# Counting edges on 128 partitions in 157 tiles, instead of 125 partitions in 160 tiles

## The reference

```python
edge_index = jnp.stack([src, dst])
h = jnp.maximum(_layernorm(x, axis=-1), 0.0)
x = x + _L0_gnn_ref(h, edge_index, ...)      # agg = segment_sum(h[src], dst, num_segments=625)
...
x = x + _L1_gnn_ref(h, edge_index, ...)      # agg = segment_sum(h[col], row)
x = x + _L2_gnn_ref(h, edge_index, ...)      # 4 blocks of attention over the edges, and an MLP each
x = x + _L3_gnn_ref(h, edge_index, ...)      # 2 layers of attention over the edges, norms and an MLP
```

## Time and profile before

| | us |
|---|---|
| median of 3 runs (1119.16 to 1120.65) | 1120.2 |
| span of the profiled execution, first to last instruction | 1117.2 |
| first matmul of the counting | 6.08 |
| first matmul of the network behind the counting (L1220) | 123.50 |
| PE busy over the span | 1066.1 (95%) |

### The profile page before, as it was taken

The page is one execution under the profiler, slowest core; times in us unless marked ns, Lnnn a source line. Parts: engine busy times, 40 slices in busy tenths (PEclk is TensorE's granted clock), DMA queues, the critical chain, the costliest instruction groups (busy, mean ns, idle before and its releaser), DMA issues.

```text
span 1117.2 us, 20722 instructions
## 1 busy us (share of the span) xinstructions
PE 1066.1 (95%) x6808; PEld 987.7 (88%) x6808; DVE 773.4 (69%) x1535; ACT 577.6 (52%) x1032; POOL 673.3 (60%) x923
## 2 busy tenths in 40 slices
PE   7999999899999999999999999999999999999797
PEld 7899897699888999889998899987999879998795
DVE  7899867756658566575665756666778867777634
ACT  7999675455321553315543145433667637676340
POOL 3232447754577545875558755499656866478671
PEclk9999999999999999999999999999999999999899
DMA  5200011412021120211201212122201201021101
GB/s 129 31 1 1 7 38 58 149 58 86 1 86 49 58 86 1 78 56 59 86 1 55 78 48 77 69 83 75 66 1 43 71 4 45 1 76 39 38 1 46
DMA packets 40963, 56.92 MB, mean 51 GB/s; under 512 B 14312, under 2 KB 14812, under 8 KB 40735
## 3 DMA queue, kind: packets, MB, share of 16 engines
q1 hardware_dynamic: 40600, 55.37, 15.7%
q10 hardware_dynamic: 260, 0.21, 0.1%
HBM read 51.44 MB, written 4.12 MB: 50 GB/s over the span
## 4 chain that ended last, share of the span: by engine, by line
PE 79%; DVE 6%; POOL 5%; ACT 4%; issue 3%; DMA 2%; DVEq 0%; POOLq 0%; SPq 0%; PEldq 0%; ACTq 0%
PE ps L340 42%; PE ps L1768 8%; PE ps L362 8%; PE ps L786 5%; PE ps L2101 3%; PE ps L2028 3%; PE ps L2402 3%; POOL w_lo L380 2%; ACT away L737 1%; PE ps L2065 1%; PE ps L1259 1%; PE ps L1246 1%; PE ps L1742 1%; DMA w_raw<-L_gnn_wk 1%; PE ps L1220 1%
## 5 line engine op out<-in xcount | busy, mean ns | idle before, releaser
L380 POOL TENSOR_TENSOR w_lo<-w_raw,w_hi 128x512 fp32r<-128x512 f32 x152 | 204.8, 1348 | 12.7
L340 PE MATMUL ps<-yt_hi,w_hi 128*128 128x314 f32 (+2 forms) x640 | 201.8, 315 | 2.8 <-DVE yt_lo L2236 1.6
L340 PE MATMUL ps<-yt_hi,w_lo 128*128 128x314 f32 (+2 forms) x640 | 197.6, 309 | 0.0
L340 PE MATMUL ps<-yt_lo,w_hi 128*128 128x314 f32 (+2 forms) x640 | 197.3, 308 | 0.0
L459 POOL TENSOR_SCALAR prob<-prob,rinv 125x628 f32<-125x628 f32 x160 | 126.4, 792 | 105.2 <-DVE rinv L444 86.9
L403 ACT ACTIVATE pt_hi<-ps 125x625 fp32r<-125x625 f32 x160 | 109.2, 694 | 102.9 <-PE ps L362 101.7
L377 POOL TENSOR_SCALAR w_hi<-w_raw 128x512 fp32r<-128x512 f32 x152 | 97.7, 643 | 95.3 <-DMA w_raw<-L_gnn_wo 28.8
L340 PEld LDWEIGHTS ps<-yt_hi,w_hi 128*128 128x128 f32 x640 | 121.8, 190 | 5.9 <-issue 4.4
L340 PEld LDWEIGHTS ps<-yt_hi,w_lo 128*128 128x128 f32 x640 | 121.7, 190 | 0.0
L340 PEld LDWEIGHTS ps<-yt_lo,w_hi 128*128 128x128 f32 x640 | 121.5, 190 | 0.1
L786 PE MATMUL ps<-oh_s,oh_d 125*125 125x314 bf16 x800 | 111.4, 301 | 10.1 <-DVE oh_s L639 6.8
(11 more groups left out here) (325 smaller groups left out, 2787.2 us busy)
## 6 DMA issues: line engine op xcount, KB each, us to landing
w_raw<-L_gnn_m_w SPq DMA_DIRECT2D x8, 1024.0 KB, 5.4
w_raw<-L_gnn_W SPq DMA_DIRECT2D x6, 1024.0 KB, 5.4
w_raw<-L_gnn_wv SPq DMA_DIRECT2D x4, 1024.0 KB, 6.1
w_raw<-L_gnn_wq SPq DMA_DIRECT2D x4, 1024.0 KB, 5.4
w_raw<-L_gnn_wk SPq DMA_DIRECT2D x4, 1024.0 KB, 7.4
w_raw<-L_gnn_wo SPq DMA_DIRECT2D x4, 1024.0 KB, 6.4
w_raw<-L_gnn_Wv SPq DMA_DIRECT2D x2, 1024.0 KB, 5.5
w_raw<-L_gnn_Wq SPq DMA_DIRECT2D x2, 1024.0 KB, 5.6
```

Of the source, the lines that this page charges most:

```text
L340: ins = pe.matmul(out_ap, lhs(i, kk), rhs(j, kk), start=kk == 0 and n == 0, stop=kk == count - 1 and n == 2)
L380: pool.tensor_tensor(w[slot][1][:, kk, 0:cols], w_raw[slot][:, kk, 0:cols], w[slot][0][:, kk, 0:cols].bitcast(FP32), ALU.subtract).then_in ...
```

## The change

The lists are laid on 128 partitions. The first 127 get 157 edges each, 19939 in all, and the last one gets the other 61. The tiles are 128 x 160 still, but the columns 0, 1 and 2 are skipped: the first chunk begins at tile 3. So there are 157 tiles, and 29 of them in the first chunk.

- Each list is loaded by two DMAs on the queue that had one: 127 partitions x 157 columns (rows of 628 bytes), and 5 overlapping pieces of 32 entries into the last partition.
- Pads and repetitions in the last partition are marked: POOL makes a tile `absent` (a memset and an `affine_select`), which is 0 for an edge that counts and -1256 elsewhere. DVE adds it to `dst_i` while it makes `dstf`, by a `scalar_tensor_tensor` that takes the place of a `tensor_copy`. A pad's `oh_d` is then zero.
- ACT has the places 0, 2, 4, 6 of each group and DVE 1, 3, 5, 7 as well as all `oh_d`. With tile 3 as the first, DVE makes the first `oh_s` as it did before.
- All one-hots are 128 partitions high. The waits on used tiles are shifted by 3 tiles. POOL's eight numbers stay as they are, and count from tile 3.
- `offset` becomes -0.497 for -0.49.

```diff
-ET = E // R
 CHUNKS = 5
-CT = ET // CHUNKS
+EP = 128
+CT = 32
+ET = CHUNKS * CT
+FULL = -(-E // EP)
+SKIP = ET - FULL
+FRESH = 12
...
-    OHA = (1, 3, 5, 7)
+    OHA = (0, 2, 4, 6)
+    USED = slice(SKIP, ET)
...
+    def edge_rows(name):
+        return a[name][0:(EP - 1) * FULL].rearrange("(p t) -> p t", t=FULL)
+
+    def edge_row(name):
+        return bass.AP(a[name].tensor, LAST_ROW, [[E, 1], [FRESH, CHUNKS], [1, CT]])
...
     def count_sp(sp):
-        sp.dma_start(ids[0][:], a["src"].rearrange("(p t) -> p t", t=ET)).then_inc(s_dst, 16)
+        sp.dma_start(ids[0][0:EP - 1, USED], edge_rows("src")).then_inc(s_dst, 16)
+        sp.dma_start(chunked(ids[0][EP - 1:EP, :]), edge_row("src")).then_inc(s_dst, 16)
         sp.dma_start(x[:], a["x"].rearrange("(t p) f -> p t f", p=R)).then_inc(s_x0, 16)
...
     def count_act(act):
-        act.dma_start(ids[1][:], a["dst"].rearrange("(p t) -> p t", t=ET)).then_inc(s_ids, 16)
+        act.dma_start(ids[1][0:EP - 1, USED], edge_rows("dst")).then_inc(s_ids, 16)
+        act.dma_start(chunked(ids[1][EP - 1:EP, :]), edge_row("dst")).then_inc(s_ids, 16)
...
+        steps.done(pool.memset(absent[:], 0.0))
         steps.wait(pool)
+        pool.affine_select(out=chunked(absent[:]), in_=chunked(absent[:]), compare_op=ALU.is_ge, fill=-2.0 * W,
+                           base=8 * CT * (EP - 1) - 8 * REAL, pattern=[[-1, CHUNKS], [8, CT]],
+                           channel_multiplier=-8 * CT).then_inc(s_absent, 1)
...
     def count_dve(dve):
-        dve.wait_ge(s_ids, 16)
-        steps.done(dve.tensor_scalar(upper[:], ids[1][:], float(H2), None, ALU.is_ge))
-        dve.wait_ge(s_dst, 16)
-        dve.tensor_copy(dstf[:], ids[0][:]).then_inc(s_idf, 1)
+        dve.wait_ge(s_ids, 32)
+        steps.done(dve.tensor_scalar(upper[:, USED], ids[1][:, USED], float(H2), None, ALU.is_ge))
+        dve.wait_ge(s_dst, 32)
+        dve.wait_ge(s_absent, 1)
+        dve.scalar_tensor_tensor(out=dstf[:, USED], in0=absent[:, USED], scalar=1.0, in1=ids[0][:, USED],
+                                 op0=ALU.mult, op1=ALU.add).then_inc(s_idf, 1)
...
         for c in range(CHUNKS):
-            for o in range(OH):
+            for o in range(0 if c else SKIP, OH):
                 onehots(c * CT + o, o, c == 0)
```

More of the change, by code:

```diff
@@ L467, in build @@
     cnt_i = cnt[:].bitcast(I32)
[L468 to L473, removed]
-    OH = 8
-    oh_d = sb("oh_d", "qk", [R, OH, W], BF16, 1280)
-    oh_s = sb("oh_s", "qk", [R, OH, H2], BF16, 1280 + OH * W * 2)
-    OHA = (1, 3, 5, 7)
-    nsrcm = sb("nsrcm", "rows", [R, ET], FP32, 4480)
-    nsrcv = sb("nsrcv", "rows", [R, ET], FP32, 5120)
-    away = sb("away", "qk", [R, len(OHA), H2], BF16, 1280 + OH * W * 2 + OH * H2 * 2)
+    ids = [sb(n, "rows", [EP, ET], I32, skip) for n, skip in (("dst_i", 0), ("src_i", 640))]
+    dstf = sb("dstf", "rows", [EP, ET], FP32, 1280)
+    srcm = sb("srcm", "rows", [EP, ET], FP32, 2560)
+    srcv = sb("srcv", "rows", [EP, ET], FP32, 3200)
+    upper = sb("upper", "rows", [EP, ET], FP32, 3840)
+    node = sb("node", "qk", [EP, W], FP16)
+    OH = 8
+    oh_d = sb("oh_d", "qk", [EP, OH, W], BF16, 1280)
+    oh_s = sb("oh_s", "qk", [EP, OH, H2], BF16, 1280 + OH * W * 2)
+    OHA = (0, 2, 4, 6)
+    USED = slice(SKIP, ET)
+    SKIP_A = sum(o in OHA for o in range(SKIP))
+    SKIP_D = 2 * SKIP - SKIP_A
+    LAST_ROW = E - (CHUNKS - 1) * FRESH - CT
+    REAL = (EP - 1) * FULL - LAST_ROW
+    assert REAL == CT - FRESH - 1 and LAST_ROW >= 0
+    nsrcm = sb("nsrcm", "rows", [EP, ET], FP32, 4480)
+    nsrcv = sb("nsrcv", "rows", [EP, ET], FP32, 5120)
+    away = sb("away", "qk", [EP, len(OHA), H2], BF16, 1280 + OH * W * 2 + OH * H2 * 2)
     offset = sb("offset", "rows", [R, 1], FP32, 5760)
+    absent = sb("absent", "ot", [EP, ET])
     above = sb("above", "ot", [R, TILES, H2], I16)
@@ L571, in count_pool @@
         steps.done(pool.memset(neg_half[:], -0.5))
-        steps.done(pool.memset(offset[:], -0.49))
+        steps.done(pool.memset(offset[:], -0.497))
         steps.done(pool.memset(neg_one[:], -1.0))
@@ L634, in onehots @@
             if not first:
-                dve.wait_ge(s_ohu, tile - OH + 1)
+                dve.wait_ge(s_ohu, tile - (OH + SKIP - 1))
             dve.tensor_scalar(oh_d[:, o, :], node[:], dstf[:, bass.ds(tile, 1)], None,
@@ L680, in count_dve @@
             for o in range(OH):
-                onehots(c * CT + OH + o, o, False)
+                onehots(c * CT + OH + o, o, c == 0 and o < SKIP)
                 norms = NORM_AT.get(c, ())
@@ L728, in move, with onehots @@
                                scale=1 / PACK).then_inc(s_above, 1)
-        def onehots(c, j, first=False, which=range(len(OHA))):
+        def onehots(c, j, which=range(len(OHA))):
             for n in which:
                 o = OHA[n]
-                tile, nth = j * OH + (c * CT + o), j * len(OHA) + (c * (CT // OH) * len(OHA) + n)
+                tile = j * OH + (c * CT + o)
+                nth = j * len(OHA) + (c * (CT // OH) * len(OHA) + n - SKIP_A)
+                first = c == 0 and tile < OH + SKIP
                 if not first:
@@ L740, in onehots @@
                 if not first:
-                    act.wait_ge(s_ohu, tile - OH + 1)
+                    act.wait_ge(s_ohu, tile - (OH + SKIP - 1))
                 act.activation(oh_s[:, o, :], away[:, n, :], ACT.Relu, bias=srcv[:, bass.ds(tile, 1)],
@@ L745, in count_act @@
         for c in range(CHUNKS):
-            onehots(c, 0, c == 0, range(2))
+            onehots(c, 0, range(0 if c else SKIP_A, 2))
             if c > 0:
                 move(c - 1)
-            onehots(c, 0, c == 0, range(2, len(OHA)))
+            onehots(c, 0, range(2, len(OHA)))
             onehots(c, 1)
@@ L778, in count_pe, with ready @@
         GROUPS = CT // OH
[L780 to L783, removed]
+        def ready(c, j, o, by_act_too=True):
+            pe.wait_ge(s_oh, j * before[-1] + (c * GROUPS * before[-1] + before[o] - SKIP_D))
+            if by_act_too:
+                pe.wait_ge(s_oha, j * by_act[-1] + (c * GROUPS * by_act[-1] + by_act[o] - SKIP_A))
         def count(c, o, m, start=False, stop=False):
@@ L795, in count_pe @@
             FREE = range(3) if c else range(TILES)
-            for o in range(2):
-                ready(c, 0, o)
+            head = 0 if c else SKIP
+            for o in range(head, head + 2):
+                ready(c, 0, o, by_act_too=c > 0 or o > SKIP)
                 for m in FREE:
-                    ins = count(c, o, m, start=o == 0)
+                    ins = count(c, o, m, start=o == head)
             if c > 0:
@@ L805, in count_pe @@
             ins.then_inc(s_ohu, 2)
-            for o in range(2, OH):
+            for o in range(head + 2, OH):
                 edge_tile(c, 0, o)
@@ L813, in count_pe @@
                     edge_tile(c, GROUPS - 1, o, o == OH - 1)
-                pe.wait_ge(s_ohu, (c + 1) * CT)
+                pe.wait_ge(s_ohu, (c + 1) * CT - SKIP)
                 pe.sem_inc(s_cf, TILES)
```

14 lines of the change are left out of this document (8 added, 6 removed).

## The result

| | before | after |
|---|---|---|
| median, us (5 runs each on one chip) | 1120.05 | 1127.06 |
| lowest to highest | 1119.16 to 1120.65 | 1126.44 to 1129.5 |
| first matmul of the counting | 6.08 | 13.76 |
| first matmul behind the counting | 123.50 | 129.26 |
| span of the profiled execution | 1117.2 | 1127.7 |

The ratio is 1.0067 (95% interval 1.0056 to 1.0078): 7.0 us slower, where 4.4 were forecast. The profiled execution is after's slowest, 1129.5 us. Three terms carry the difference.

A forecast was written before the change was run, and what follows sets the result against it. PE's counting, behind a list load nothing can bypass, was taken as the bound. -2.0 + 5.85 + 0.1 + 0.08 + 0.2 + 0.13 = +4.4 us on 1117.2 gives 1121.6, plus 3.0 to the median: 1124.6; range 1122.0 to 1128.0.

The forecast's parts named there:

- hurt chunk ends: Rival: list late as forecast, and `w_lo` against `unpack` at three chunk ends costs up to 2.7 us; 1127.3; chance 0.10.
- dear rows: In the chunk-ends rival: list rows on the one engine at 0.032 us or above, giving 1128.2; that rival's chance 0.10.
- The three tiles, -2.0: In the first chunk of the counting: 15 matmuls fewer at 0.133 us each, all on the path, -2.0 us.
- The lists in 127 rows, +5.85: At the start: both lists go through one DMA engine, 254 rows at 0.0287 us, 7.29 us for 1.44.
- two bounds of this term: Load of the lists: +4.9 us with a row at 0.025 us, +6.7 with a row at 0.032.
- x and the weights behind it: Loads after the lists: x and weights land about 5.9 us later, as the counting does, so they cost nothing.
- The small transfers and the pads: At the start: each list's second transfer +0.1 us; DVE's `scalar_tensor_tensor` in place of `tensor_copy` +0.08 us.
- The ends of chunks, +0.2: Fifth tile's `oh_s` now comes from ACT behind `move`: four places at 0.05 us, +0.2 us (0 to 0.4).
- the last `oh_s`, +0.13: End of the counting: ACT's last `oh_s` is now the last tile but one's, so one more matmul follows the wait.
- POOL's pieces, 0: POOL's pieces come one tile before chunk ends rather than four, `w_lo` beside `unpack`: nothing; other end +2.7 us.
- C: Experiments' theory: PE's idle time behind the counting, at a certain time behind PE's start, sets off the half clock.

The follow-up runs named there:

- 113 + 12 rows: Kernel before, 125 partitions and 160 tiles, each list loaded in two transfers of 113 and 12 rows: 1126.7 us, ratio 1.0066.
- two of 157 tiles with filler: Changed kernel with lists in 112 + 15 rows, plus 12 useless matmuls in PE's idle time behind the counting, run twice: 1117.76 and 1118.01 us.
- two of before with filler: Kernel before with 12, then 6, useless matmuls in PE's idle time behind the counting: 1122.16 us with 12, 1120.79 with 6.
- before again: Kernel before, unchanged, measured and profiled a second time: 1119.7 us.
- after again: Changed kernel, nothing further altered, measured and profiled a second time: 1127.9 us, ratio to before 1.0076.
- 112 + 15 rows: Changed kernel, but each list's 127 rows go in two transfers, of 112 and 15 rows: 1119.49 us, ratio to before 1.0002.
- the same, POOL's numbers: Changed kernel with lists in 112 + 15 rows, plus POOL's eight numbers of used tiles 3 lower: 1118.91 us, ratio to before 0.9997.
- x behind both lists: Changed kernel, but SP waits for both lists before it issues the load of x: 1125.75 us, ratio to before 1.0057.
- 15 matmuls ahead: Changed kernel with lists in 112 + 15 rows, plus 15 useless matmuls ahead of the counting's last 8 tiles: 1121.5 us, ratio 1.0017.

## Why the prediction was right, and where it was off

The time after, 1127.06, lies in the range of 1122.0 to 1128.0, and the sign was given 0.86. The forecast was 1124.6. The sign is right for the reason given, the lists on one DMA engine. That the time is still in the range is partly luck: its upper part was meant for hurt chunk ends and dear rows, and neither came. Two costs that no term and no rival has, 1.6 and 1.5 us, fill it instead. By its steps:

- **The three tiles, -2.0.** Right: 785 matmuls at the old pace. The first chunk, 21.59 us for 23.82 up to ACT's first `move`, is -2.2, and in the second executions -1.4 (22.18 for 23.55), but the difference lies in PE's first microseconds, which the prediction didn't look at. There a matmul comes every 0.26 us, and only later every 0.13. Before, its start and a stretch soon after:

```profile
6.20:9.20 3.00, 3.00 (x11) 2.29 (x12) 3.00 (x7) 2.85 (x6) 2.42 (x14) 1.00 0.33 124
10.20:13.20 3.00, 3.00 (x24) 3.00 (x23) 2.95 (x11) 2.91 (x6) 0.00 (x0) 1.00 0.32 122
```

  11 matmuls in 3 us is the pace of the half clock, though the row says 1.00 (the trace's record of the clock begins only with its rise). The rise comes at another time in every execution: 3.4 to 5.7 us behind PE's first matmul. At 3.6 us behind it, in the first and in the second execution of after:

```profile
17.40:18.40 1.00, 1.00 (x9) 1.00 (x8) 1.00 (x5) 0.97 (x3) 0.00 (x0) 1.00 0.07 25
17.60:18.60 1.00, 1.00 (x5) 0.87 (x5) 1.00 (x5) 0.97 (x3) 0.00 (x0) 1.00 0.07 25
```

  Half of the time up to the rise is lost. With that half taken off, the first chunk is 21.8 us in the three profiles of 160 tiles in the table below and 19.8 in its six of 157: -2.0.
- **The lists in 127 rows, +5.85.** Right in its rule and in its price: one engine, share 0.07, and DVE's first step at 10.52 when nothing is in the way. The rows start off 256-byte boundaries, for which an estimate from the Trainium skill (DMA: Bandwidth & Descriptors, section "How a descriptor splits into AXI transactions") gave 0.5 us more. The 10.52 for 10.5 shows no such cost here, and neither does the kernel with 113 + 12 rows: from 5.3 to 7.9 us its `src` rows of 640 bytes start every 0.061 us, and after's of 628 bytes every 0.060. The two bounds of this term are uneven: they change the price of a row after and leave the 1.44 us before as they are. With one price for both they are +5.0 and +6.5, not +4.9 and +6.7. And the forecast's own range, 1122.8 to 1126.6, is wider than these bounds and the chunk ends give (1123.4 to 1125.7).
- **x and the weights behind it, "Nothing".** This step failed. It says that x has its rows "behind the list", and that is so on SP's queue. But the later list is on ACT's, and there x isn't behind it but beside it, on the one engine that both need. The prediction had noted that the lists of the two queues share an engine, and didn't ask the same of x. It also took it that "the first list is hardly complete before the second"; but `src`, with its head start, has its last row at 9.09 us and `dst` at 11.34, and these rows are the ones that x delays. +1.6 us. The weights themselves were issued at 20.72, as forecast (20.8), since the engine's work as a whole was counted rightly.
- **The small transfers and the pads, +0.1 and +0.08.** PE started 7.68 us later and DVE 7.60, so 0.08 is the step of the pads. The small transfers can't be told from the rest.
- **The ends of chunks, +0.2, and the last `oh_s`, +0.13.** Right: from `move` to `move` the chunks take 22.89, 23.23 and 22.93 us for 22.89, 23.14 and 22.85, and from the last `move` to the first network 24.86 for 24.72. Together +0.3.
- **POOL's pieces, 0.** Right, as the end of the third chunk shows, to be held against the earlier trace rows:

```profile
81.47 2.18 ACT L757 ACTIVATE above<-ps,offset 125x314 int16<-125x314 f32 x5 [0.27 <-PEq L848]
81.59 1.26 POOL L384 TENSOR_TENSOR w_lo<-w_raw,w_hi 128x512 fp32r<-128x512 f32 x1
...
82.02 2.14 DVE L678 SCALAR_TENSOR_TENSOR below<-above,ps 125x314 int16<-125x314 int16 x5 [1.78 <-ACT above L757]
82.97 3.04 PEld L818 LDWEIGHTS ps<-oh_s,oh_d 128*125 128x125 bf16 x23 [0.64 <-DVE below L678]
```

  `w_lo` now runs beside `unpack`, which takes 2.14 us for five as it did (2.13). The rival that feared 2.7 us here falls.
- **What was in no term:** the half clock behind the counting, +1.5 us. The prediction took PE's pace behind the counting as given. In the profile of before the idle time is there, and the clock behind it is at 1.00.

The two misses are 3.1 us together, and the forecast lacks 2.5. Against them stand 0.2 us of PE's first microseconds, 0.3 between the two profiles and the medians, and 0.15 between the median that the forecast started from (1120.2) and before's 1120.05.

What is left is why the clock falls there in one kernel and not in the other. Six profiles of kernels with 157 tiles and the idle time show it. None of the three with 160 tiles and the same idle time does. The two of 157 tiles with filler don't show it (the two of before with filler say nothing on it, since there is no fall to prevent). The time from PE's start doesn't decide it, nor does the start itself, since 113 rows made PE nearly as late as 127. But the traces divide if one counts from the clock's rise in PE's first microseconds (us; the rise as in the trace's record of the clock):

| profile | rise behind PE's first matmul | idle time, counted from the rise | fall, counted from the rise |
|---|---|---|---|
| before | 3.97 | 111.5 to 113.5 | none |
| before again | 3.42 | 111.8 to 113.8 | none |
| 113 + 12 rows | 4.35 | 111.3 to 113.2 | none |
| after | 3.52 | 110.0 to 112.0 | 112.6 |
| after again | 4.72 | 109.4 to 111.4 | 112.6 |
| 112 + 15 rows | 3.66 | 110.0 to 111.9 | 112.6 |
| the same, POOL's numbers | 3.87 | 109.8 to 111.8 | 112.6 |
| x behind both lists | 4.66 | 109.4 to 111.4 | 112.6 |
| 15 matmuls ahead | 5.42 | 110.5 to 112.5 | 112.6 |

The fall comes at one and the same time behind the rise in all six, and PE is back from its idle time before it. In the three others PE is still idle at that time. This also says why the 15 matmuls didn't help: they moved the idle time by 2.3 us against PE's start, but the rise came 1.8 us later in that execution. So C may be right with the rise in the place of PE's start. This is read from nine profiles and tested by none: no kernel of 157 tiles had its idle time as late as the three of 160, nor one of 160 as early, so that anything else in which the two groups differ, such as one-hots of 128 rows, could be the reason as well. Each kernel stood in one or two traces only, and the medians say that the cost is real (1.7 us between the kernel of 112 + 15 rows and its filled version), not in how many executions it comes. And the stops at the turns of the loop, some 1 to 1.5 us each, are seen but not explained.

## What to carry to other kernels

Count the rows of a transfer before you count its bytes: a tile of 128 partitions loaded as 127 + 1 can cost more than three tiles of work save, and 112 + 15 + 1 gives it back. Where two queues share a DMA engine, ask of every transfer that is on it at the time, not only of those ahead in the same queue, whether its rows come between yours. Where PE comes out of an idle time into the next stage, look at the granted clock of the first microseconds there, since it can take what was won in front of it. And before a difference of some tenths between two profiles is put down to an edit, look at when PE's pace rises in either.

## What the runs showed of the hardware that was not expected

- Two queues with work for one DMA engine took turns row by row, so the one with the large rows got most of the time: a list's rows of 628 bytes came every 0.10 us beside rows of 2 KB, and every 0.06 us beside the other list's.
- The granted clock fell to 0.50 for 3.4 us, 0.1 to 1.3 us after PE had come back from an idle time of 2 us, in six of six profiles of kernels with 157 tiles and in none of three with 160 tiles and the same idle time. In the six it fell 112.6 us behind its rise. Twelve useless matmuls in the idle time kept it at 1.00, in both profiles with them.
- PE began the counting at a matmul every 0.26 us, and went over to 0.13 after 3.4 to 5.7 us, in every execution at another time. This alone makes up to 1.1 us between two executions.
- The same program has 1.4 us more at a turn of a loop in one execution than in another (41.77 and 40.32 us), with PE waiting for nothing that the profile shows.
